# A graph network kernel: empty slots masked on VectorE, setup reordered around the early gathers, and the counting stage written as a straight program over edges re-read in step order

## The reference

```python
def L0(feat, efeat, W_msg, b_msg, W_attn, b_attn, src, dst):      # edge-wise attention
    w_m = (efeat @ W_msg + b_msg).reshape(E, 16, 16)
    w_a = (efeat @ W_attn + b_attn).reshape(E, 16, 16)
    h_src = feat[src][:, :, None]
    e1, e2 = w_m * h_src, w_a * h_src
    ex = exp(e2 - segment_max(e2, dst)[dst])
    attn = ex / segment_sum(ex, dst)[dst]
    return segment_sum(e1 * attn, dst).sum(axis=1)
def gin_conv(x, src, dst, eps, wa, ba, wb, bb):
    h = (1.0 + eps) * x + segment_sum(x[src], dst)
    return relu(h @ wa + ba) @ wb + bb
def L1(x): return log_softmax(gin_conv(relu(gin_conv(x, ...1)), ...2))
x = layernorm(x + L0(x, edge_attr, ...))
x = layernorm(x + L1(x))
```

## Time and profile before

| | |
|---|---|
| median of 3 runs | 3278.06 us (3277.54 to 3279.08) |
| the profiled execution | 3278.26 us, span 3276.4 us |
| busy in the span | DVE 2407.7 us (73%), PE 2002.4 (61%), POOL 1396.3 (43%), ACT 1223.8 (37%) |
| chain that ended last, by engine | POOL 33%, issue 25%, DVE 11%, PE 10%, ACT 9%, DMA 5% |
| costliest line of that chain | POOL h_stage L506, 22% |
| granted TensorE clock | 0.899 of full speed |

### The profile page before, as it was taken

How to read it: one execution, slowest core, us unless ns; L and a number is a source line. 1 busy time by engine, 2 the same in 40 slices (tenths; PEclk the granted TensorE clock), 3 DMA queues, 4 the chain that set the end, 5 groups by cost and what they waited for, 6 DMA issues and landing times.

```text
span 3276.4 us, 43067 instructions
## 1 busy us (share of the span) xinstructions
PE 2002.4 (61%) x6488; PEld 811.5 (25%) x6489; DVE 2407.7 (73%) x3809; ACT 1223.8 (37%) x2426; POOL 1396.3 (43%) x1327
## 2 busy tenths in 40 slices
PE   0000677777777777777888305665366666656688
PEld 0000233333333333333333102222022111212233
DVE  3442788888888888888899698889887666656610
ACT  2120233333333333333333003333387777767712
POOL 8877777888778778888754000000000000000000
PEclk9999999999999999989999758999699889888887
DMA  3322122222222222222211104665000000000000
GB/s 120 124 95 82 41 59 59 55 59 53 58 60 53 58 59 54 57 57 57 66 57 54 67 0 142 184 182 147 0 2 1 1 1 1 1 2 1 1 1 3
DMA packets 113369, 178.30 MB, mean 54 GB/s; under 512 B 44014, under 2 KB 71254, under 8 KB 112078
## 3 DMA queue, kind: packets, MB, share of 16 engines
q1 hardware_dynamic: 68930, 109.55, 10.2%
q0 software_dynamic: 37840, 40.09, 6.4%
q10 hardware_dynamic: 6456, 27.40, 2.1%
HBM read 106.02 MB, written 71.23 MB: 54 GB/s over the span
## 4 chain that ended last, share of the span: by engine, by line
POOL 33%; issue 25%; DVE 11%; PE 10%; ACT 9%; DMA 5%; DVEq 3%; ACTq 2%; SPq 1%; POOLq 0%
POOL h_stage L506 22%; ACT hot_sq L1006 4%; ACT hot_lo L1010 4%; DMA md<-group_sums 3%; POOL hb L552 3%; POOL blk L548 3%; PE quad L812 3%; PE quad L774 2%; DVE mt L1286 2%; PE bank L740 2%; POOL hb L576 2%; POOL hb L572 1%; DVE em L1223 1%; PE bank L673 1%; DVEq L319 1%
## 5 line engine op out<-in xcount | busy, mean ns | idle before, releaser
L673 PE MATMUL bank<-em,identf 128*128 128x512 f32 x1776 | 932.2, 629 | 89.0 <-ACT spb L924 89.0
L506 POOL DMA_INDIRECT h_stage<-in_x,src_ring x784 | 884.0, 1128 | 232.9 <-issue 227.4
L1223 DVE TENSOR_TENSOR em<-quad,hb 128x1024 f32<-128x1024 f32 x444 | 526.1, 1215 | 201.7 <-PE quad L663 143.0
L774 PE MATMUL quad<-hot_key,hot_lo 128*128 128x500 bf16 x1260 | 434.5, 407 | 229.3 <-ACT hot_lo L1010 135.7
L1410 DVE TENSOR_SCALAR hot_key<-iota_key,w,kb 128x500 bf16<-128x500 f16 x1260 | 467.4, 406 | 33.4 <-PE quad L774 18.5
L673 PEld LDWEIGHTS bank<-em,identf 128*128 128x128 f32 x1776 | 326.7, 199 | 354.9 <-issue 267.0
L1006 ACT ACTIVATE hot_sq<-iota_lo,minus_lo 128x128 bf16<-128x128 f16 x840 | 289.4, 392 | 133.4 <-issue 84.2
L663 PE MATMUL quad<-wst,eft 100*128 100x512 bf16 x888 | 276.7, 417 | 47.8 <-DVE em L1223 47.6
L913 ACT ACTIVATE em<-em 128x1024 f32<-128x1024 f32 x222 | 229.6, 1053 | 159.4 <-DVE em L1260 155.0
L1231 DVE TENSOR_TENSOR em<-em 128x1024 f32<-128x1024 f32 x222 | 280.5, 1264 | 0.0
L1260 DVE TENSOR_TENSOR em<-em,spb 128x1024 f32<-128x1024 f32 x222 | 267.8, 1247 | 3.8
(11 more groups left out here) (255 smaller groups left out, 2164.5 us busy)
## 6 DMA issues: line engine op xcount, KB each, us to landing
md<-group_sums SPq DMA_DIRECT2D x136, 384.0 KB, 3.1
group_sums<-spb SPq DMA_DIRECT2D x111, 384.0 KB
edge_rows<-rows ACTq DMA_DIRECT2D x8, 2441.4 KB
h_stage<-in_x,src_ring POOLq DMA_INDIRECT x784
h_rows<-h_stage SPq DMA_DIRECT2D x98, 64.0 KB, 2.4
ef_in<-in_edge_attr ACTq DMA_DIRECT2D x8, 781.2 KB
fence<-fence_d SPq DMA_DIRECT2D x1, 3840.2 KB, 11.6
blk<-edge_rows,est_i POOLq DMA_INDIRECT x97, 3.4
```

The costliest lines, as they stand in the source:

```text
L506: pool.indirect_dma_start(h_stage[:, k, j, :], None, x, bass.IndirectOffsetOnAxis(ap=src_ring[:, c % 2, n % HCH, j:j + 1], axis=0)).then_i ...
L673: mm = pe.matmul(bank[5][:, :], identf[:, :], em[:, b, j, :, :, :].rearrange("p i a o -> p (i a o)"), start=(j == 0), stop=(j == G - 1))
L774: pe.matmul(bank[b % 4][:, 0:CW], hot_lo[:, q, :], hot_key[:, q, :], start=False, stop=False).then_inc(hot_used, 1)
L1223: dve.tensor_tensor(em[:, b, 2 * q:2 * q + 2, :, :, :].rearrange("p j i a o -> p (j i) (a o)"), quad[:, 2 * q % 4:2 * q % 4 + 2, :].rearra ...
```

## The change

1. POOL no longer masks. `real` and `empty` become one tile `gate` (1.0 where the slot is empty, about -3e38 where it is real), and DVE raises the slots of step t+1 with one maximum inside step t, just before it subtracts the step's maximum. ACT's flag is the Relu of `gate`. `fetch_late` waits for the buffer's former DMAs.
2. Setup: HPRE goes from 19 to 9, the ring HST from 3 to 5, and 89 blocks instead of 79 are gathered during the 96 steps. POOL reads `srow` before it gathers anything. SP has fewer `keep_h` between the table DMAs.
3. `er` is read in step order by 24 indirect DMAs of POOL, from DRAM copies `dst_rows` and the new `src_rows`; an iteration that serves a window gets its own row, so an edge unit that touches two windows is read twice. DVE works out the rows' numbers (`past_win`, `unit_i`) and takes the window's offset off the keys.
4. Counting: DVE builds all `hot_lo` and `hot_key` with one pointer scalar each, in 420 x 3 pairs written out without a loop or register. ACT only copies windows. PE keeps its loops and its load of 17 registers. The dense window's counts are copied out in f32 by ACT, and DVE marks them after the last window. `ut` is filled after counting.

```diff
-HST = 3
+HST = 5
-HPRE = 19
+HPRE = 9
@@ setup, SP
-            for n in range(5):
-                keep_h(n)
             sp.wait_ge(start_kept, 1)
...
-            keep_h(5)
             sp.wait_ge(start_out, 32)
...
-            for n in range(6, 10):
+            for n in range(5):
                 keep_h(n)
             sp.wait_ge(row_ready, 1)
...
-            for n in range(10, 12):
+            for n in range(5, 6):
                 keep_h(n)
             sp.wait_ge(scattered, 16 * NT)
...
-            for n in range(12, 14):
+            for n in range(6, 7):
                 keep_h(n)
             sp.wait_ge(owner_ready, 1)
@@ setup, POOL
-            for n in range(3):
-                collect(n)
             pool.wait_ge(rows_found, 1)
...
-            for n in range(3, 11):
+            for n in range(6):
                 collect(n)
...
-            collect(11)
             pool.wait_ge(scatter_ready, 1)
...
+            pool.wait_ge(units_ready, 1)
+            pool.wait_ge(src_out, 64)
+            for c in range(RC):
+                for q in range(EU):
+                    for k, ids in enumerate((src_rows, dst_rows)):
+                        pool.indirect_dma_start(er[:, k, c, q * P:(q + 1) * P], None, ids.rearrange("r (h e) -> (r h) e", e=P),
+                                                bass.IndirectOffsetOnAxis(ap=unit_i[:, c, q:q + 1], axis=0)).then_inc(er_in, 16)
-            for n in range(12, HPRE):
+            for n in range(6, HPRE):
                 collect(n)
@@ level 1
-            return min(NBLK, HPRE + 5 * t // 6)
+            return min(NBLK, HPRE + 89 * t // 96)
...
                 fetch_early(t + 1)
-                raise_empty(t, t % 3, t // 3)
                 for n in range(blocks_by(t), blocks_by(t + 1)):
                     collect(n)
@@ DVE, step
+            def raise_empty(t, b, i):
+                dve.wait_ge(h_in[b], 16 * (i + 1))
+                dve.nop(nofuse=True)
+                dve.tensor_tensor(hb[:, b, :, :], hb[:, b, :, :],
+                                  gate[:, bass.ds(t * G, G)].unsqueeze(2).to_broadcast([P, G, F]), ALU.max).then_inc(h_ready, 1)
...
+                raise_empty(t + 1, (b + 1) % 3, i if b < 2 else i + 1)
                 dve.wait_ge(max_taken, 4 * t + 4)
@@ counting, DVE
+            for r in range(RT):
+                for q in range(EU):
+                    ge(dve, hot_used, EU * (r - 1) + q + 1)
+                    dve.tensor_scalar(hot_lo[:, q, :], iota_lo[:, :], lo_s[:, q, r:r + 1], None, ALU.is_equal)
+                    dve.tensor_scalar(hot_key[:, q, :], iota_key[:, :], key_s[:, q, r:r + 1], None,
+                                      ALU.is_equal).then_inc(hot_ready, 1)
@@ counting, PE
-                    with pe.Fori(units[b], units[b + 1] + 1) as i:
+                    with pe.Fori(iters[b], iters[b + 1]) as r:
                         for q in range(EU):
-                            if q == 1:
-                                pe.wait_ge(lo_ready, i + w + 2)
-                            pe.wait_ge(hot_ready, EU * (i + w) + q + 1)
+                            pe.wait_ge(hot_ready, EU * r + q + 1)
```

More of the change, by code:

```diff
@@ L380, in _ @@
             sp.dma_start(own_p[:, :], owner_d[0:S].rearrange("(t p) -> t p", p=P)).then_inc(owner_in, 16)
-            keep_h(14)
+            for n in range(7, 8):
+                keep_h(n)
             sp.wait_ge(fence_ready, 1)
@@ L389, in spill @@
                 sp.dma_start(group_sums[bass.ds(t, 1)].rearrange("a p c -> p (a c)"), spb[:, b, :]).then_inc(spill_out[b], 16)
-            for n in range(15, HPRE):
+            for n in range(8, HPRE):
                 keep_h(n)
@@ L558, in fetch_early, with fetch_late @@
                     pool.wait_ge(h_out[t % HST], 16 * (t // HST + 1))
-                fetch(t, t % 3, est_i[:, t:t + 1], HBLK * (t + 1 if t < NBLK - 2 else NBLK))
-            def fetch_late(t, b):
+                fetch(t, t % 3, est_i[:, t:t + 1], HBLK * (t + 1 if t < NBLK else NBLK))
+            def fetch_late(t, b, i):
+                pool.wait_ge(blk_in[b], 16 * i)
+                pool.wait_ge(h_in[b], 16 * i)
+                pool.nop(nofuse=True)
                 pool.tensor_copy(estc[:, b:b + 1], est_i[:, bass.ds(t, 1)]).then_inc(pool_step, 1)
@@ L616, in _ @@
             pe.transpose(bank[1][0:NT, 0:P], start_nm[:, :], identf[:, :]).then_inc(start_turned, 1)
+            pe.wait_ge(row_ready, 1)
+            pe.matmul(bank[7][:, 0:NW + 1], ones_row[0:1, :], r_row[0:1, :], start=True, stop=True).then_inc(iters_bcast, 1)
             pe.wait_ge(nm_in, 64)
@@ L1398, in windows @@
-            def windows(v, units, dense, first=False):
-                for b in range(WG):
-                    w = WG * v + b
-                    with dve.Fori(units[b], units[b + 1] + 1) as i:
-                        for q in range(EU):
-                            dve.wait_ge(hot_used, EU * (i + w) + q + 1)
-                            dve.nop(nofuse=True)
-                            if q == 0:
-                                dve.tensor_scalar(hot_lo[:, 0, :], iota_lo[:, :], minus_lo[:, bass.ds(EU * i, 1)], 0.0,
-                                                  ALU.add, ALU.is_equal)
-                            dve.tensor_scalar(hot_key[:, q, :], iota_key[:, :], w500[:, bass.ds(w, 1)],
-                                              kb[:, bass.ds(EU * i + q, 1)], ALU.add, ALU.is_equal).then_inc(hot_ready, 1)
-                    if b == 0 and not first or b > 0 and dense:
-                        keep_left(w - 1, (b + 3) % 4)
-                    if b == 0 and not dense:
-                        dve.sem_inc(left_past, WG - 1)
@@ new lines, in _ @@
+            dve.wait_ge(win_ev, NW)
+            with dve.Fori(0, hw) as w:
+                dve.wait_ge(left_or, w + 1)
+                dve.nop(nofuse=True)
+                dve.scalar_tensor_tensor(out=left_any[:, :].rearrange("p (n h) -> p n h", h=NT),
+                                         in0=cnt[:, :, bass.ds(w * WIN, WIN)].rearrange("p h n -> p n h"), scalar=float(EXACT),
+                                         in1=left_any[:, :].rearrange("p (n h) -> p n h", h=NT),
+                                         op0=ALU.is_ge, op1=ALU.max).then_inc(left_or, 1)
```

240 lines of the change are left out of this document (115 added, 125 removed).

## The result

The changed kernel takes **3074.12 us** (median of 4 runs, 3073.37 to 3074.58) against 3278.57 us (3277.54 to 3279.88) for the kernel before on the same chip: a ratio of 0.9376, 95% interval 0.936 to 0.9392. The forecast was 3094 us, with a range of 3035 to 3185.

A forecast was written before the change was run, and what follows sets the result against it. The prediction took POOL to bound level 1's 96 steps, DVE its last steps, and DVE's operations and stops counting. Its terms summed as 3278 - 48 + 24 + 3 - 166 + 3 = 3094 us, range 3035 to 3185.

The forecast's parts named there:

- Setup, -48 forecast: Setup up to POOL's first fetch: 325.6 - 128 + 35 + 31 + 14 = 278 us; -48 us, bounds -60 and -30.
- The other chain: In setup, the tables' chain (scatter, table back, owners, fences, `er` operations beside them) ends near 275 us, 303.7 before.
- The 96 steps, +24 forecast: Level 1's 96 written steps: masks gone -134 us, ten more blocks +110, fetches without lead +48; +24 us together.
- The waits without lead: From step 83 of the 96, each fetch waits for the block just gathered: 3.7 us, 13 times, 48 us.
- the price of an operation of DVE beside POOL: In the 96 steps, DVE's new maximum costs POOL 0.06 us a step, 5 us in all, left inside the rounding.
- The last steps, +3 forecast: Level 1's last 15 steps, bound by DVE: 0.29 us more each, less DVE's loss to POOL's masks; +3 us (0 to +5).
- Counting, -166 forecast: Counting: 0.43 us a pair, 542 us for 420 iterations, 622 us in all against 789; -166 us.
- 6 + 50 + 14 + 10: Counting, beside the pairs: PE's first register load 6 us, nine later loads 50, PE's lower clock 14, late PE restarts 10.
- The rival in which the second pointer is free: Counting: a second pointer costs nothing, so 0.49 us a pair, -90 in place of -166, 3170 us; chance 0.12.
- That overlap is lost: Rival, counting: DVE operations no longer overlap, 0.66 us a pair, kernel slower than before at 3380 us; chance 0.08.
- After counting, +3 forecast: After counting: filling `ut` (0.9 us) and marking the dense window stand on the path; +3 us.
- the one without a gain in setup: Rival, setup: tables chain stays late, DMAs queue behind the 2.4 MB `edge_rows` writes, no gain; 3135 us; chance 0.08.

The follow-up runs named there:

- e6_block6: Changed kernel with POOL gathering block 6 while it waits for the scatter's indices in setup, instead of after the `er` gathers: 3067.25 us, ratio 0.9357.
- e8_swap: Changed kernel with DVE making the fences before the seven operations on `er` instead of behind them: 3077.09 us.
- e2_lead: Changed kernel with the 89 blocks gathered at a steeper rate, 9 + 24 t / 25 instead of 9 + 89 t / 96: 3038.24 us, ratio 0.9267.
- e1_masks_pool: Changed kernel with the two masks per step back on POOL, DVE's maximum left out and a gather ring of four slots instead of five: 3199.78 us, ratio 0.9758.
- e9_two_maxima: Changed kernel with DVE's maximum done twice in every step of level 1, once into a spare tile nobody reads: 3084.21 us.
- e3_two_pointers: Changed kernel with a second pointer scalar on `hot_key` in counting (a zero added before the comparison): 3143.15 us.
- e14_act_less: Kernel before with ACT making one of its two Square operations an iteration in counting (counts wrong): 3199.65 us against 3277.4, ratio 0.9765.
- e4_loop: Changed kernel with DVE's 1260 pairs of counting in a loop of 420 passes of three pairs, row index in a register: 3140.09 us.
- e11_lead_block6: Changed kernel with both the steeper gathering rate and block 6 gathered during the wait for the scatter: 3040.43 us, ratio 0.9273.

## Why the prediction was right, and where it was off

It was right in its sign, its range and its main term, and 20 us too high. By stages it was 8.5 and 3 us too low, then 15, 13 and 4 too high, so part of the nearness is luck.

**Setup, -48 forecast, -39.5 measured.** The shifts were right in kind, two in size. The chain of `row_ready` moved up by 19 us (174.2 to 155.1), not 29, and the scatter's indices came at 183.5 instead of 177. POOL was ready at 170 instead of 163, since its 48 gathers ahead of the scatter took 1.93 us each (73.8 to 166.2) and not 1.60; that it idled 14.4 us as forecast is luck, both ends lay 7 us late. From the indices to the first fetch it took 102.5 us for 101. So the late indices are nearly the whole miss. The other chain was late by as much: the tables were ready near 282.9, not 275. The prediction let the `er` chain run beside the fences and had no term for the 11.6 us that the last read of `er` takes to land; but in the changed kernel POOL's own gathers came 3 us after it (e6_block6, e8_swap), so that this cost nothing.

**The 96 steps, +24 forecast, +27.0 measured.** The waits without lead are as worked out, 13 of them, 46.1 us for 48, and in e2_lead they are gone; the prediction missed the fourteenth, 3.3 us, at the end of the stage. The masks are 1.40 us a step (e1_masks_pool). Three small terms were missing. Gathers went from 1.38 to 1.41 us in the first 1000 us and to 1.39 over the stage (1.33 behind 1300 us), some 7 us; two long ones took 9 more; and fetches went from 3.04 to 2.93 us a step, 11 us less. What failed inside this stage is the price of an operation of DVE beside POOL. The prediction took 0.06 us a step, 5 us in all, from the mean of all operations, against 28 for a POOL that is held up for the whole length; e9_two_maxima has 0.16 a step, 15 us, for a second maximum. That the stage came out only 3 us off is in part luck, for the cheaper fetches paid for it.

**The last steps, +3 forecast, -12.1 measured.** This step failed, and in its sign. The prediction added 0.29 us for the maximum and called what DVE had lost to POOL's masks small. DVE's step fell from 11.92 (in the mean) to 11.41 us with one operation more, and rises to 11.88 with the masks back. e9_two_maxima prices the maximum there at 0.20 us, so some 1.6 us of masks on POOL cost DVE 0.47 + 0.20 = 0.67 us a step. 15 x 0.51 = 8 us of the 12; the other 4 lie at the border of the stages and are not settled.

**Counting, -166 forecast, -179.3 measured.** The price of what is there now was right: 0.42 for 0.43 us a pair, PE's gaps as before, DVE's waits for them 73.6 us for the forecast 6 + 50 + 14 + 10. Inside that sum the parts were less good. DVE covers 0.6 us of a gap, not 1.3, and gets its first buffer back 1.0 us after PE's restart (2434.6 to 2435.2 and 2441.1 to 2442.1, with PE's clock at 0.50 of full speed from 2441.1 to 2444); this makes 68 us at the nine gaps for 50 + 14, and the 10 us for windows in which PE restarts late hardly exist.

The rival in which the second pointer is free would have added 76 us to the forecast; e3_two_pointers shows that it costs 69. That overlap is lost did not happen: `hot_lo` starts before `hot_key` has ended. The 0.15 us between them in the kernel before were mostly ACT's pace: with ACT relieved they are 0.05, in the same loop (e14_act_less). A loop adds a gap of its own, 0.09 us in e4_loop, and the straight program has none.

What was wrong is the account of before. The prediction took DVE's operations and stops for the bound and saw no engine over 72%. ACT set most iterations, 1.51 us, with its copy of a window (0.57) on top; e14_act_less gains 78 us by relieving it alone. DVE's work for an iteration hardly changed with the edit, 1.25 us then (three keys with two pointers, one `hot_lo`) and 1.27 now (three pairs with one pointer). The rest of the gain, about 100 us, is idle time of DVE: 191 us before `hot_lo` with ACT relieved, 74 now. Of it the ten stops between groups of windows were 120 us and are some 70, now that DVE neither loads registers nor jumps there; the others are short waits at the windows. In the kernel before the chain runs through one such stop of DVE, from 2870.5 to 2883.7: 6.1 us of issue around its branches and 6.4 us of loading registers, where PE's own load had begun 5 us earlier (2871.8 against 2876.8). This split is read from the traces; no run puts DVE's register loads or its window loops back alone. The forecast was safe from this, since it was summed from what comes and not from what goes.

**After counting, +3 forecast**, below +1 measured. Among the rivals, the one without a gain in setup adds up to 3094 + 48 = 3142 us, not 3135.

## What to carry to other kernels

Build a forecast of a rewritten stage from the operations that will be there, and look at the old bound engine by engine over two successive iterations, not by its busy share: ACT was busy 72% of the stage and yet set most iterations, through 0.3 us between its operations. When a buffer stock is meant to run down over a stage, keep its lead at one or more to the end: here a schedule with the same number of blocks, only at a slightly steeper rate, gives 36 us (the two long gathers that are missing there may have a part in it). Where two engines hinder each other, as POOL and DVE do here, an operation taken off one can give time to both; it is worth reading the partner's step where the partner alone is the bound.

## What the runs showed of the hardware that was not expected

- A pass of six short DVE operations in a loop took 1.43 us where the operations need 1.27, and 1.47 where they need 1.44: with longer operations the loop costs 0.03 us a pass instead of 0.16.
- A load of registers on PE costs an estimated 0.34 us a register and 0.8 us besides (gaps of 2.45 us for 5 and 6.49 us for 17), and DVE, which fills PE's buffers, loses 0.4 to 0.7 us more than the gap (2.9 and up to 7.2 us), in spite of three buffers.
- Two maskings on POOL of together 1.6 us lengthen a DVE step of 11.41 us by 0.67 us (e1_masks_pool, e9_two_maxima).
- In the 96 steps of the changed kernel one gather kept POOL for 6.73 us and the fourth behind it for 4.30, where 0.94 is the rule. A gather of 6.5 to 7.1 us comes back between 1401 and 1419 us in all seven experiments that leave level 1 as it is, with one of 4.30 behind it in most, and in none that alters the steps of level 1 (e1_masks_pool, e2_lead, e9_two_maxima, e11_lead_block6), nor before. No run here explains it:

```profile
1402.93 6.73 POOL h_stage L521
1409.66 0.30 issue
1409.96 0.94 POOL h_stage L521
```
